# A Mamba block with routed experts on one core: norm offsets, slots and the second weight on GpSimd, residual sums by identity products, the logarithm's mask on ScalarE

## What is computed

```
n0 = layernorm(x)                       # offset = -mean * rstd, "x_one" in the kernel
a  = n0 + mamba(ln(n0) * g1 + b1)       # "x_two"
     # in mamba: delta = softplus(dt @ dt_w.T + dt_b)
     #           = max(pre, 0) + log1p(exp(-|pre|))
     #           h = exp(delta*A) * h + delta*B*xc ;  y = sum over 16 states of h*C
f  = a + silu(gate) * val @ ffp_w.T + ffp_b
x  = x + f                              # "x_four"
m  = layernorm(x)                       # "m_tok"
logits = m @ Ws + bs ; top 2 of 8 ; softmax of the two
x  = x + sum of the two experts' outputs, weighted
```

## Time and profile before

| | us |
|---|---|
| median of 3 runs | 910.73 |
| lowest, highest | 905.72, 913.05 |
| the profiled execution, its own time | 908.7 |
| the profiled execution, span from first to last instruction | 906.5 |

### The profile page before, as it was taken

How to read it: one execution, slowest core, us unless ns; L and a number is a source line. 1 busy time by engine, 2 the same in 40 slices (tenths; PEclk the granted TensorE clock), 3 DMA queues, 4 the chain that set the end, 5 groups by cost and what they waited for, 6 DMA issues and landing times.

```text
span 906.5 us, 13029 instructions
## 1 busy us (share of the span) xinstructions
PE 669.6 (74%) x3684; PEld 487.7 (54%) x3684; DVE 735.0 (81%) x1135; ACT 496.7 (55%) x1070; POOL 575.0 (63%) x488
## 2 busy tenths in 40 slices
PE   4467578778767786797789778877885586888964
PEld 1144244445335544683477347734773375787963
DVE  1378879989998999979998999999999985453463
ACT  3447676766776576546745665657554442422421
POOL 1185556566756895799778976898579825335422
PEclk9669699799979987898799969988897788988997
DMA  7833133223312336532653355336543534447693
GB/s 180 242 116 108 47 96 114 84 64 112 119 39 93 100 112 187 160 112 97 192 148 107 99 173 158 118 88 182 154 130 112 167 100 125 132 126 200 183 309 112
DMA packets 96458, 120.07 MB, mean 132 GB/s; under 512 B 11463, under 2 KB 63507, under 8 KB 96371
## 3 DMA queue, kind: packets, MB, share of 16 engines
q1 hardware_dynamic: 91843, 109.86, 41.6%
q0 software_dynamic: 4544, 9.38, 2.8%
HBM read 107.20 MB, written 16.34 MB: 136 GB/s over the span
## 4 chain that ended last, share of the span: by engine, by line
PE 25%; DVE 20%; issue 12%; ACT 6%; DMA 2%; SPq 2%; another core or an unknown queue 1%; POOL 0%; DVEq 0%; ACTq 0%; POOLq 0%
DVE state L951 10%; PE gate L1250 3%; PE up L1268 2%; DVE product L961 2%; PE up L1257 2%; PE y L1156 2%; PE y L1151 2%; PE work_front L1107 2%; PE work_front L1113 1%; ACT decay L815 1%; DVE stats L881 1%; DVE silu_m L1072 1%; DVE x_tok L990 1%; PE decay L1250 1%
## 5 line engine op out<-in xcount | busy, mean ns | idle before, releaser
L696 POOL TENSOR_TENSOR inflow<-du,b_wide 128x1024 f32<-128x1024 f32 x128 | 317.3, 2482 | 177.5 <-DVE product L961 116.9
L951 DVE TENSOR_TENSOR_SCAN state<-decay,carry,inflow 128x512 f32<-128x512 f32 x192 | 235.1, 1266 | 4.2 <-ACT decay L815 4.0
L815 ACT ACTIVATE decay<-delta,a_neg 128x512 f32<-128x512 f32 x256 | 172.1, 690 | 113.6 <-DVE state L951 107.2
L961 DVE TENSOR_TENSOR product<-state,c_wide 128x1024 f32<-128x1024 f32 (+1 forms) x105 | 144.8, 1379 | 4.8 <-PE y L1151 3.4
L723 POOL DMA_INDIRECT y_dram<-y_rows,x_rows x78 | 87.6, 1123 | 93.5 <-ACT y_rows L871 86.3
L1151 PE MATMUL y<-ident,product 128*128 128x128 f32 x748 | 111.7, 294 | 42.5 <-DVE product L961 42.5
L1151 PEld LDWEIGHTS y<-ident,product 128*128 128x128 f32 x748 | 91.9, 152 | 80.4 <-DVE product L961 50.1
L1156 PE MATMUL y<-h_rows,ident 128*128 128x512 f32 x138 | 90.2, 773 | 28.5 <-ACT h_rows L780 28.5
L717 POOL DMA_INDIRECT row_dram<-m_tok,place x64 | 72.6, 1134 | 24.6 <-issue 14.6
L951 DVE TENSOR_TENSOR_SCAN state<-decay,inflow 128x512 f32<-128x512 f32 x64 | 74.7, 1211 | 9.6 <-ACT decay L815 7.0
L1107 PE MATMUL work_front<-u_t,w_tap 128*128 128x512 f32 x128 | 65.7, 641 | 6.0 <-ACT u_t L751 4.4
(11 more groups left out here) (210 smaller groups left out, 1274.4 us busy)
## 6 DMA issues: line engine op xcount, KB each, us to landing
b_wide<-bc_dram SPq DMA_DIRECT2D x128, 256.0 KB
c_wide<-bc_dram SPq DMA_DIRECT2D x105, 256.0 KB
w_stage<-gate_up_dram SPq DMA_DIRECT2D x78, 344.0 KB
x_rows<-row_dram SPq DMA_DIRECT2D x78, 65.0 KB
x_tok<-in_x SPq DMA_DIRECT2D x8, 256.0 KB, 5.9
out<-x_tok SPq DMA_DIRECT2D x8, 256.0 KB
inflow<-y_dram SPq DMA_DIRECT2D x6, 256.0 KB, 4.0
gate_up_dram<-in_Wg SPq DMA_DIRECT2D x1, 1376.0 KB, 9.2
```

The source lines that it names most:

```text
L696: e.tensor_tensor(inflow[:, key % 3], du[:, c % 2], b_wide[:, key % ROW_SLOTS:key % ROW_SLOTS + 1, :].to_broadcast([P, HALVES, CHUNK]), AL ...
L815: e.activation(decay_bank[h][:], delta[:, c % 2, h, :], ACT.Exp, scale=a_neg[:, h, n:n + 1]).then_inc(S["decay"], 1)
L951: e.tensor_tensor_scan(state[:, key % STATE_SLOTS, h, :], decay_bank[h][:], inflow[:, key % 3, h, :], 0.0 if c % (SEQ // CHUNK) == 0 else ...
L961: e.tensor_tensor(product[:, key % 2, :, :wide], state[:, key % STATE_SLOTS, :, :wide], c_wide[:, key % ROW_SLOTS:key % ROW_SLOTS + 1, :wi ...
```

## The change

1. The three offsets go from VectorE to GpSimd, each as two instructions (times -1, times rstd) right behind its rstd. The rows `shift0`, `shift2`, `shift3` leave the tables.
2. `place` goes to GpSimd at the same place of the order, as five instructions: the product, three halving sums in the stead of the reduction, the cast. The second weight (L1033) goes to GpSimd, ahead of `tag0`.
3. `x_two` and `x_tok` are added in PSUM by two more products of `ff_out` with the identity, 128x512 each; `x_four` is a single copy from PSUM to SBUF.
4. The mask is made by ScalarE as relu(1 - 64*x), in the unit behind `series`; the predicated copy moves with it, from the unit of FRONT's row 13 to that of row 14. The square moves from ahead of the logarithm into row 13's unit. Ahead of the logarithm a table set is named that holds both the logarithm and the exponential.

```diff
@@ FRONT, BACK
-    (("tanh_z1",), ("shift0", "silu1"), ("x_one",)),
+    (("tanh_z1",), ("silu1",), ("x_one",)),
...
-    ((), ("c_rows", "series", "small", "log1p"), ()),
-    ((), ("delta",), ()),
+    (("square",), ("c_rows", "series"), ()),
+    (("small",), ("log1p", "delta"), ()),
...
-    ((), ("shift2",), ("n_tok",)),
+    ((), (), ("n_tok",)),
...
-    ((), ("shift3",), ("m_tok",)),
+    ((), (), ("m_tok",)),
@@ gpsimd
+            def norm_shift(slot, key):
+                e.tensor_scalar(shift[:, slot, :], mean_var[:, slot, :, 0], -1.0, None, ALU.mult).then_inc(S[f"shift{slot}"], 1)
+                e.wait_ge(S[f"shift{slot}"], 2 * key + 1)
+                e.tensor_tensor(shift[:, slot, :], shift[:, slot, :], rstd[:, slot, :], ALU.mult).then_inc(S[f"shift{slot}"], 1)
...
+                    e.wait_ge(S["rstd0"], 6 * key + 2)
+                    norm_shift(0, key)
...
+                    e.wait_ge(S["rstd2"], 2 * key + 2)
+                    norm_shift(2, key)
...
+                    e.wait_ge(S["rstd3"], 2 * key + 2)
+                    norm_shift(3, key)
...
+                elif name == "place":
+                    e.wait_ge(S["count"], 2 * key + 1)
+                    e.tensor_tensor(picked[:], rank[:].rearrange("p (o s) e -> p o s e", o=1).to_broadcast([P, TOPK, SUB, EXPERTS]), choice[:],
+                                    ALU.mult).then_inc(S["place"], 1)
+                    e.wait_ge(S["place"], 5 * key + 1)
+                    e.tensor_tensor(picked4[:], picked[:, :, :, 0:4], picked[:, :, :, 4:8], ALU.add).then_inc(S["place"], 1)
+                    e.wait_ge(S["place"], 5 * key + 2)
+                    e.tensor_tensor(picked2[:], picked4[:, :, :, 0:2], picked4[:, :, :, 2:4], ALU.add).then_inc(S["place"], 1)
+                    e.wait_ge(S["place"], 5 * key + 3)
+                    e.tensor_tensor(place_f[:], picked2[:, :, :, 0], picked2[:, :, :, 1], ALU.add).then_inc(S["place"], 1)
+                    e.wait_ge(S["place"], 5 * key + 4)
+                    e.tensor_copy(place[:, key], place_f[:]).then_inc(S["place"], 1)
...
-                        e.wait_ge(S["weights"], 3 * (key + 1))
+                        e.wait_ge(S["weights"], 2 * (key + 1))
+                        e.tensor_tensor(tag[:, 1, key * SUB:(key + 1) * SUB, 0].bitcast(f32), top_w[:, 0, :],
+                                        tag[:, 0, key * SUB:(key + 1) * SUB, 0].bitcast(f32), ALU.mult).then_inc(S["tag0"], 1)
@@ scalar
                 elif name == "log_dt":
                     e.wait_ge(S["exp_dt"], 2 * key + 2)
...
+                    e.preload_act_table_set("natural_log_exp_and_others")
+                    e.activation(du[:, key % 2], exp_dt[:], ACT.Ln, bias=1.0).then_inc(S["log_dt"], 1)
+                elif name == "square":
+                    e.wait_ge(S["exp_dt"], 2 * key + 2)
...
                     e.activation(ser_dt[:], exp_dt[:], ACT.Square, bias=ser_shift[:], scale=LOG1P_SCALE).then_inc(S["ser0"], 1)
...
+                elif name == "small":
+                    e.wait_ge(S["log_dt"], key + 1)
+                    e.wait_ge(S["series"], key + 1)
+                    e.activation(exp_dt[:], exp_dt[:], ACT.Relu, bias=1.0, scale=-64.0).then_inc(S["small"], 1)
@@ vector
-                    e.tensor_tensor(x_two[:], x_two[:], side[:].rearrange("p (s d) -> p s d", s=SUB), ALU.add).then_inc(S["x_three"], 1)
-                    e.wait_ge(S["x_three"], key + 1)
-                    e.tensor_tensor(x_tok[:, key], x_two[:], x_tok[:, key], ALU.add).then_inc(S["x_four"], 1)
+                    e.tensor_copy(x_tok[:, key], side[:].rearrange("p (s d) -> p s d", s=SUB)).then_inc(S["x_four"], 1)
@@ tensor
                     e.matmul(side[:], ones[0:1, :], b_ffp[:].rearrange("o s d -> o (s d)"), start=True, stop=False, skip_group_check=True)
+                    e.matmul(side[:], ident[:], x_two[:].rearrange("p s d -> p (s d)"), start=False, stop=False, skip_group_check=True)
+                    e.matmul(side[:], ident[:], x_tok[:, key].rearrange("p s d -> p (s d)"), start=False, stop=False, skip_group_check=True)
```

More of the change, by code:

```diff
@@ L112 @@
 LOG1P_REST = 1.0 - LOG1P_SHIFT ** 2
-HEAD = ["stats0", "rstd0", "rstd1", "shift0", "x_one", "prepare", "u_tok", "u_turn", "u_t", "halo", "in0a", "in0b", "conv0", "in1a", "in1b",
-        "conv1", "tanh_c", "xc", "x_proj", "x_dbl", "dt0", "pre_dt0", "dt1", "pre_dt1", "exp_dt", "log_dt", "c_turn", "c_rows", "series", "small", "log1p",
+HEAD = ["stats0", "rstd0", "rstd1", "x_one", "prepare", "u_tok", "u_turn", "u_t", "halo", "in0a", "in0b", "conv0", "in1a", "in1b",
+        "conv1", "tanh_c", "xc", "x_proj", "x_dbl", "dt0", "pre_dt0", "dt1", "pre_dt1", "exp_dt", "log_dt", "square", "c_turn", "c_rows", "series", "small", "log1p",
         "delta", "du"]
@@ L468, in mamba_moe_block @@
             + ["out_proj", "x_two", "n_tok", "n_turn", "n_t", "ff_gate", "gate_evac", "ff_val", "silu_g", "ff_h", "ff_out"]
-            + ["x_three", "x_four", "m_tok", "m_turn", "m_t", "route", "top", "gap", "route_exp", "top_if", "choice", "both", "weights"]
+            + ["x_four", "m_tok", "m_turn", "m_t", "route", "top", "gap", "route_exp", "top_if", "choice", "both", "weights"]
             + ["rank", "count", "place"]
@@ L714, in _ @@
                     if s == 0:
-                        e.wait_ge(S[f"tag{q}"], c + 1)
-                        e.wait_ge(S["place"], 3 * (c + 1))
+                        e.wait_ge(S[f"tag{q}"], c + 1 if q else 2 * (c + 1))
+                        e.wait_ge(S["place"], 5 * (c + 1))
                     e.indirect_dma_start(row_dram, bass.IndirectOffsetOnAxis(place[:, c, q, s:s + 1], 0),
@@ L884, in norm_stats @@
                     e.bn_aggr(mean_var[:, slot, s, :], stats[:, slot, s, :]).then_inc(S[f"aggr{slot}"], 1)
-            def norm_shift(slot):
-                e.scalar_tensor_tensor(shift[:, slot, :], mean_var[:, slot, :, 0], -1.0, rstd[:, slot, :], ALU.mult, ALU.mult).then_inc(S[f"shift{slot}"], 1)
             for name, key in order:
@@ L1017, in _ @@
                     if key:
-                        e.wait_ge(S["place"], 3 * key)
+                        e.wait_ge(S["place"], 5 * key)
                     for q in range(TOPK):
@@ L1212, in _ @@
                     e.wait_ge(S["m_tok"], SUB * (key + 1))
[L1213 removed]
+                    e.wait_ge(S["x_four"], key + 1)
                     transposes(side, m_tok[:, key % M_SLOTS], "m_turn")
```

43 lines of the change are left out of this document (10 added, 33 removed).

## The result

| | before | after |
|---|---|---|
| median of 20 runs each, us | 907.0 | 918.1 |
| lowest, highest | 904.4, 915.2 | 908.5, 923.8 |
| span of the profiled execution | 906.5 | 921.9 |

The ratio is 1.0078, with a 95% interval of 1.0052 to 1.0104. It leaves out the 4 of the 20 runs after that lie more than 1.5% above the fastest one, the profiled one among them, which is why it is smaller than the ratio of the medians in the table, 1.012. The forecast was 914 us. The profiled execution of the changed kernel is its longest, 923.8 us by its own time, and its granted clock, 0.859 in the mean, is the lowest of the 20, whose median is 0.873. What follows from it alone overstates the loss, above all where the clock has a part, and needs a second kernel that shows the same.

A forecast was written before the change was run, and what follows sets the result against it. Waits were taken to end with GpSimd in late chunks' units 1 to 9, VectorE in 9 to 16, mixed early. Late chunks +6.0, early -5.4, end +2.5, together +3.1 us on 908.7 (2 below median): 914 us, range 893 to 930.

The forecast's parts named there:

- Held time passes on: VectorE: some 37 of 57.8 us busy is standing behind GpSimd and mostly passes to the next instruction with two SBUF inputs.
- Units 1 to 9 of a late chunk: Stretch of 46.0 us in the five chunks from about 297 us; its getting shorter would show the forecast wrong.
- units 15 to 8: Late chunk: GpSimd runs 3 to 3.5 us late by unit 1, VectorE level until about unit 7; +0.7 us.
- the late chunk's `x_four`: Unit 9: two products start it 2.1 us later; loss 1.3 us without a hold, gain about 0.8 with; -0.2 us.
- The offsets: Six GpSimd instructions a chunk at 0.20 us each, within about 4 us a chunk added there, 32 over the run.
- the rival that wanted 0.5 us each: The slower rival, GpSimd the bound, is right if GpSimd's small steps take 0.5 us or more each; chance 0.30.
- The mask: Units 10 and 11: early chunks gain 1.8 to 3 us; late ones lose 0 to 1.7 by a held copy, +0.7.
- The table loads: ScalarE, ahead of unit 10's decay: the second load (1.28 us) is moved to stand before a tanh, not gone.
- The end and the start: Behind the last scan: identity products, longer offsets and slot steps add 2.5 us (0 to 5); no start term.
- VectorE the bound everywhere: Faster rival: own time and some holds go, 36 us, `x_four` takes back 16; 20 us less, 891; chance 0.28.
- GpSimd the bound from unit 15 to 11: Slower rival, late chunks: GpSimd's 4 us per chunk come through, 20 us for five; +19, about 929; chance 0.30.
- The change does nothing to the loop: Rival: loop stretches are long by alternation alone, only the end grows; 913; chance 0.42 together with the forecast.

The follow-up runs named there:

- only_identity: Kernel before with only the residual sums moved to TensorE as identity products: 911.8 us, ratio 1.0033.
- only_place: Kernel before with only the slots and the second weight moved to GpSimd: 912.7 us, ratio 1.0063.
- all_but_identity: The full change, but x_four is again two additions on VectorE: 909.8 us, ratio 1.0019 to the kernel before.
- all_but_offsets: The full change, but the norm offsets stay on VectorE: 910.4 us, ratio 1.0012 to the kernel before.
- only_offsets: Kernel before with only the three norm offsets moved to GpSimd: 914.4 us, ratio 1.0106.
- only_mask: Kernel before with only the mask on ScalarE, the square's new place and the table set: 906.2 us, ratio 0.9958.
- mask_late_load: only_mask without the early load of the exp and ln table: 904.8 us, ratio 0.9934 to the kernel before.
- mask_same_unit: mask_late_load with the predicated copy and the ReLU back in row 13's unit: 917.0 us, ratio 1.0092 to the kernel before.
- offsets_none: Kernel before with the norm offsets zero for good, L887 gone and nothing in its place: 906.2 us, ratio 0.9952.
- offsets_both: Kernel before with L887 kept and two unused GpSimd steps added behind each rstd: 912.4 us, ratio 1.0045.
- offsets_both_wait: offsets_both with x_one, n_tok, m_tok waiting for the two steps, and GpSimd not waiting for its own second step: 920.4 us, ratio 1.0122 to before.

## Why the prediction was right or wrong

**The sign and size.** The ratio lies within 1% of no change, as forecast, though its interval reaches to 1.0104. The median of 918 us lies in the range and 4 us above the forecast. That flatters it: the forecast stood on a median before of 910.7 us, and in the comparison that median was 907.0. Of the change itself I had foreseen 3 us, and 0.78% is 7, more than double. The direction and the kind of the terms came out, some of the sizes didn't.

**Held time passes on: right for the whole, and more than said.** Of the signs named, the copy is held (mean 1.94 us, I had said it passes 2), the products with C are longer (1379 to 1677 ns), and `xc` is held where L887 went. I had let part of the 37 us of holds vanish, behind L990 and L1053, and put VectorE's fall at 35 to 58 us. It was 7 us. Taken alone the parts differ: behind L990 the held time goes (only_identity, above), behind L1053 it doesn't (only_place takes groups of 15.4 us away, and VectorE falls by 1.9). Two smaller signs missed: GpSimd gained its 96 instructions but 16.2 us and not 20 to 30, and VectorE waited 1 to 2 us ahead of `x_four` in two chunks of eight, 0.5 to 0.7 in three and 4.1 to 7.1 in three. The tile scatter's issues passed 1.8 us 12 times of 78, for 9 before.

**Units 1 to 9 of a late chunk.** I had named as a sign of being wrong that this stretch gets shorter. Cut at the inflows, as the earlier trace rows has it, three of the five late chunks are 0.7 to 0.9 us shorter there and two 0.3 to 0.9 longer. From VectorE's first scan of unit 1 to that of unit 9 all five are longer, by 3.4, 1.1, 2.0, 0.9 and 2.0 us. The sign depended on where the stretch was cut, and it can't be held for or against the argument. By the scans, which the time hangs on, the late chunks differ from the kernel before as follows; each figure is a sum over the five, from one execution of each kernel:

| us | units 0 to 8 | unit 9 | units 10 and 11 | units 12 to 15 | in all |
|---|---|---|---|---|---|
| the full change | +12.3 | +4.4 | +4.5 | -4.3 | +17.0 |
| all_but_identity | +12.1 | -1.0 | +4.6 | -5.5 | +10.2 |
| all_but_offsets | +8.5 | -2.8 | +2.0 | +1.5 | +9.2 |
| only_place | +8.0 | -0.8 | +0.1 | -2.4 | +4.8 |
| only_offsets | +4.7 | -0.1 | +1.7 | +0.5 | +6.8 |
| only_identity | +3.4 | -1.4 | 0.0 | -0.6 | +1.4 |

**The term that was too small: units 15 to 8.** I had +0.7 us a late chunk for the longer GpSimd there. Units 0 to 8 grew by 2.5 us a chunk, with the identity products and without them, and more than half of that with the slots and the weight alone. The walk through the units had VectorE level until about unit 7. By the trace its products are held more often and longer than that: the 105 of them gained 31.3 us. In part units 12 to 15 give it back, for which I had nothing.

**The term that went by one clock: the late chunk's `x_four`.** I priced the two products at TensorE's full clock only, from the earlier trace rows, as 2.1 us, and set the unit at -0.2. (The cases named there, a gain of 0.8 in three chunks and a loss of 1.3 less 0.2 in two, come to nearly nothing a chunk.) At full clock they cost 1.7 us, and in the full change VectorE waited 1.6, 0.5, 0.7 and 0.5 us in the four chunks of the loop that had it. In only_identity unit 9 of the late chunks is 0.3 us shorter in the mean, as forecast. In the full change the clock was down in three late chunks, and `ff_out` took 5.6, 7.5 and 7.5 us, VectorE's wait 1.6, 7.1 and 5.4; unit 9 changed by -0.9, +4.8 and +2.6 us. So the lower clock cost there in two chunks, and in an execution that is no typical one. The whole growth of 5.1, 6.8 and 5.2 us of these three chunks isn't its work: the first has its growth ahead of `x_four`, and all_but_identity, without the products, has late chunks that grow by 3.9, 2.3 and 4.0 us at the same places. A mean clock of 0.87 for the loop, and 0.86 for units 9 to 16, stood in the earlier trace rows; the step should have asked what the added products cost at the lower level, 2.08 us each and not 1.12.

**The offsets.** I gave them a share of the 4 us a chunk that GpSimd gets and took most of that for hidden. On their own they cost 1.06%, 9.6 us. The instructions' size was right (0.24 and 0.24 us, priced 0.20), so the rival that wanted 0.5 us each isn't what happened. The experiments put 0.45% on their time on GpSimd. For the rest they show two differences, who waits and who comes first at the copy, and don't separate them; that a shift of 0.1 us decides who is held for 2.2 us was in no term of the sum.

**The mask.** The gain was right in sign for the early chunks: they are 2.6 us shorter in the mean (1.8 predicted). For late chunks I had a loss of 0.7 us in units 10 and 11, and it was 0.9 in the full change. In only_mask, mask_late_load and all_but_offsets, where GpSimd isn't late by the offset, the copy isn't held in the late chunks (1.3 to 1.4 us in each), in all_but_identity it is (1.9 to 2.3). So the hold belongs to parts 1 and 4 together, and about half of the loss with it: without the offsets 0.4 us are left.

**The table loads: right.** I counted the second load as moved. The groups by line of the kernel after:

```profile
L826 ACT ACT_TABLE_LOAD x8 | 10.3, 1283 | 0.2
...
L842 ACT ACT_TABLE_LOAD x4 | 5.1, 1283 | 0.1
L902 ACT ACT_TABLE_LOAD x4 | 5.1, 1283 | 0.1
```

Sixteen loads, as before; the second one now stands ahead of a tanh. The Trainium skill (ScalarE: Activation LUTs, "Table sets") gives one load instead of two where a logarithm is followed by an exponential. The trace agrees for the pair: no load stands between them any more. The tanh that follows takes one again, so none is saved.

**The end and the start.** Behind the last scan 2.3 us were added (161.3 to 163.6), 2.5 predicted. That they agree is luck as much as anything: three kernels that change nothing there (only_mask, mask_late_load, mask_same_unit) lie between 156.7 and 162.0, and only_identity, which adds its products there, at 157.8. The start grew from 45.0 to 48.9 us up to the first scan, of which I had nothing; kernels that leave the start as it was are at 45.5 (only_place) and 47.1 (only_identity).

**The rivals.** *VectorE the bound everywhere* is out: 24 instructions less on it and none elsewhere (offsets_none) give 0.5%, and a gain of 2% didn't show in any part. *GpSimd the bound from unit 15 to 11* is half right. GpSimd's additions cost where they stand alone, 0.45% for the steps of offsets_both and 0.6% for only_place, and units 0 to 8 grow; as the sum of 20 us it doesn't come through, since without the offsets or without the identity products the rest of the change costs 0.1 to 0.2%. *The change does nothing to the loop* is out by only_mask and only_offsets, which move it in opposite directions.

## What to carry to other kernels

Busy time that is waiting at a shared resource isn't always removed with the instruction that shows it: look whether the next instruction stands at the same resource, and if so count the saving at undisturbed durations. Before work is put on TensorE ahead of something that waits for it, price it at the lower clock as well, and ask how often that stretch runs at it. When two experiments are compared, read the whole difference between the two kernels, waits included. A helper step that goes to another engine and back costs least when a whole unit of other work lies between its ends; here that choice was worth 1.6%, more than any of the moves themselves. The mask part with it (904.8 us, ratio 0.9934) is the version to keep of those measured, with or without the early load (0.9958).

## What the runs showed of the hardware

- Two instructions that exclude each other, 0.11 us apart in one order and 0.02 us apart in the other: the same predicated copy takes 1.32 us or 3.53 us, 2.2 us more. The Trainium skill (SBUF — State Buffer, "Who interferes with whom") calls it an exclusive lock held for the whole instruction, and the rows agree; that so small a shift decides it is what I hadn't expected.
- Whether GpSimd waits for its own last step moves the start of its next instruction by 0.12 us: 0.08 us behind that step's recorded end with the wait (offsets_both), 0.04 to 0.05 ahead of it without (offsets_both_wait, only_offsets).
- A product of 128x512 in fp32 takes 1.12 us at granted clock 1.00 and 2.08 us at 0.50. From 430 to 440 us in the kernel after the clock stayed at 0.50, with TensorE busy all the time.
